# 32 inverse square roots per row half on GpSimd: one power instruction replaced by an integer seed, a cubic correction and a Newton step

## The reference, cut to what matters

```python
def l2norm(t):
    return t / jnp.maximum(jnp.linalg.norm(t, axis=-1, keepdims=True), 1e-12)
...
def attn_layer(x, Wqkv, qs, ksc, Wo):
    qkv = x @ Wqkv
    q, k, v = jnp.split(qkv, 3, -1)          # 16 heads of 64
    q = l2norm(q) * qs
    k = l2norm(k) * ksc
    q = q * cos * scale + rotate_half(q) * sin * scale
    k = k * cos * inv + rotate_half(k) * sin * inv
    out = local_attention(q, k, v)           # windows of 32, each sees itself and the one before
    return out @ Wo

def ffn_layer(x, g, bln, W1, b1, W2, b2):
    xn = (x - mu) / jnp.sqrt(var + 1e-05) * g + bln
    hg = xn @ W1 + b1
    a, gate = jnp.split(hg, 2, -1)
    return a * jax.nn.gelu(gate, approximate=False) @ W2 + b2
...
for i in range(DEPTH):                       # 6
    x = attn_layer(shift_tokens(x), ...) + x
    x = ffn_layer(shift_tokens(x), ...) + x
```

## Time and profile before

| what | value |
|---|---|
| time, median of 3 runs | 4746.68 us (4745.28 to 4752.33) |
| time of the profiled execution | 4743.42 us |
| its span, first to last instruction | 4741.6 us |
| mean granted TensorE clock | 0.957 |
| busy: PE, PEld, DVE, ACT, POOL | 87%, 59%, 62%, 55%, 70% |
| L908, the power: 192 instructions | 1044.0 us, 5438 ns each |

### The profile page before, as it was taken

One profiled execution on the slowest core, in us unless ns is written; L12 is line 12 of the kernel. 1 busy time (PEld: TensorE's weight loads), 2 busy tenths in 40 slices (PEclk: granted clock), 3 DMA queues, 4 the chain that ended last, 5 costly groups with the idle time before them and its releaser, 6 DMA issues. The chain is left out here.

```text
span 4741.6 us, 161504 instructions
## 1 busy us (share of the span) xinstructions
PE 4145.7 (87%) x67078; PEld 2784.5 (59%) x67078; DVE 2917.3 (62%) x4217; ACT 2627.4 (55%) x4417; POOL 3317.3 (70%) x1514
## 2 busy tenths in 40 slices
PE   5878788779999999999999999999999999999994
PEld 2434344356666666666666666666666666666663
DVE  5565656556666666666666666666666666666664
ACT  2535354446556556666556555656566555655562
POOL 0000000189889888988888889988898888888891
PEclk8989888899999999999999999999999999999997
DMA  0000000112222222222222222222222222222222
GB/s 27 2 15 2 15 16 2 41 45 56 65 70 74 54 69 65 71 56 65 65 69 63 56 65 73 75 51 69 65 72 57 62 65 69 63 56 65 69 73 71
DMA packets 284546, 258.84 MB, mean 55 GB/s; under 512 B 122871, under 2 KB 258508, under 8 KB 271148
## 3 DMA queue, kind: packets, MB, share of 16 engines
q1 hardware_dynamic: 283820, 248.14, 19.5%
HBM read 117.63 MB, written 29.77 MB: 31 GB/s over the span
## 5 line engine op out<-in xcount | busy, mean ns | idle before, releaser
L783 DVE TENSOR_TENSOR products<-bank_d,table 128x1024 f32<-128x1024 f32 x772 | 937.9, 1215 | 722.5 <-ACT sq L610 696.5
L908 POOL TENSOR_TENSOR rnorm<-clamped,minus_half 128x32 f32<-128x32 f32 x192 | 1044.0, 5438 | 16.0
L903 POOL TENSOR_TENSOR products<-products 128x2048 f32<-128x2048 f32 x192 | 870.7, 4535 | 152.0 <-DVE products L783 152.0
L409 PE MATMUL bank_d<-w_qkv,xT 128*128 128x512 f32 x1544 | 806.4, 625 | 19.6 <-DVE products L783 14.7
L610 ACT ACTIVATE sq<-bank_d 128x512 f32<-128x512 f32 x772 | 467.9, 606 | 478.7 <-PE bank_d L409 468.6
L926 POOL TENSOR_TENSOR qk_rot<-products,rnorm 128x2048 f32<-128x2048 f32 x192 | 695.5, 3622 | 14.9 <-POOL rnorm L908 14.5
L870 POOL MEMSET ident<- 128x128 f32 x1 | 0.2, 205 | 917.1 <-POOLq L1044 917.1
L781 DVE TENSOR_REDUCE ss<-sq 128x16 f32<-128x1024 f32 x386 | 468.6, 1214 | 232.5 <-ACT sq L610 232.5
L933 POOL TENSOR_TENSOR prob<-prob,inv_sum 128x1024 f32<-128x1024 f32 x192 | 365.1, 1901 | 187.5 <-DVE inv_sum L763 187.5
L1471 DVE TENSOR_REDUCE part_max<-s_max 128x1 f32<-128x512 f32 (+3 forms) x768 | 398.5, 554 | 151.2 <-PE s_max L1220 100.5
L455 PE MATMUL bank_a<-ident,qk_rot 128*128 128x128 f32 x3072 | 414.7, 291 | 76.8 <-issue 64.7
(11 more groups left out here) (158 smaller groups left out, 7216.9 us busy)
## 6 DMA issues: line engine op xcount, KB each, us to landing
v_back<-v SPq DMA_DIRECT2D x96, 768.0 KB, 5.4
w_qkv<-in_Wqkv_dram SPq DMA_DIRECT2D x25, 1024.0 KB, 5.1
v_back<-v SPq DMA_DIRECT2D x192, 128.0 KB, 5.4
w_qkv<-in_Wqkv_dram SPq DMA_DIRECT2D x25, 512.0 KB, 5.4
xs<-x_layers SPq DMA_DIRECT2D x194, 64.0 KB, 2.1
w_o<-in_Wo_dram SPq DMA_DIRECT2D x24, 512.0 KB, 5.5
xr<-x_layers SPq DMA_DIRECT2D x96, 128.0 KB, 2.2
x<-x SPq DMA_DIRECT2D x96, 128.0 KB, 1.8
```

The costliest lines, as they stand in the source:

```text
L409: nc.tensor.matmul(bank[:, :], xT[:, P * a:P * (a + 1)], w_qkv[:, col:col + 512], start=True, stop=True).then_inc(d_filled if i < 8 else a ...
L783: nc.vector.tensor_tensor(products[:, a, head:head + 8, :, :].rearrange("p h r (o d) -> p h r o d", o=2), bank[:, :].rearrange("p (h r d) ...
L903: link(nc.gpsimd.tensor_tensor(products[:, a, :, 0, :], products[:, a, :, 0, :], products[:, a, :, 1, :], ALU.add))
L908: link(nc.gpsimd.tensor_tensor(rnorm[:, a, :], clamped[:, a, :], minus_half[:, :], ALU.pow))
```

## The change

`inverse_norms` gets a new body. The clamp stays. The power over 32 values of each row (L908) is replaced by eleven instructions over the same 32 values: a seed from the bits of the float (tensor_scalar on int32 views), a cubic correction (six instructions) and one Newton step (four instructions). Seven of the eleven take two tensors (tensor_tensor), four take one (tensor_scalar); all are linked one behind the other. `minus_half` shrinks to the two columns that `normalise_x1` still uses; its power (L915) stays.

```diff
-        minus_half = sb("minus_half", [P, 2 * HEADS])
+        root_t = sb("root_t", [P, 2 * HEADS])
+        root_u = sb("root_u", [P, 2 * HEADS])
+        minus_half = sb("minus_half", [P, 2])
...
             def inverse_norms(a):
 
-                link(nc.gpsimd.tensor_scalar(clamped[:, a, :], ss[:, a, :], FLT_MAX, 1e-24, ALU.min, ALU.max))
-                link(nc.gpsimd.tensor_tensor(rnorm[:, a, :], clamped[:, a, :], minus_half[:, :], ALU.pow))
+                x, r, t, u = clamped[:, a, :], rnorm[:, a, :], root_t[:, :], root_u[:, :]
+                tt, ts = nc.gpsimd.tensor_tensor, nc.gpsimd.tensor_scalar
+                link(ts(x, ss[:, a, :], FLT_MAX, 1e-24, ALU.min, ALU.max))
+                link(ts(r.bitcast(i32), x.bitcast(i32), -0.5, float(RSQRT_MAGIC), ALU.mult, ALU.add))
+
+                link(tt(t, x, r, ALU.mult))
+                link(tt(t, t, r, ALU.mult))
+                link(ts(u, t, 0.375, -1.25, ALU.mult, ALU.add))
+                link(tt(u, u, t, ALU.mult))
+                link(ts(u, u, 1.0, 1.875, ALU.mult, ALU.add))
+                link(tt(r, r, u, ALU.mult))
+
+                link(tt(t, x, r, ALU.mult))
+                link(tt(t, t, r, ALU.mult))
+                link(ts(t, t, -0.5, 1.5, ALU.mult, ALU.add))
+                link(tt(r, r, t, ALU.mult))
```

More of the change, by code:

```diff
@@ L914, in normalise_x1 @@
                 nc.gpsimd.tensor_scalar(neg_mean[:, :], mean_var[:, :, 0], -1.0, 1.0, ALU.mult, ALU.mult)
-                link(nc.gpsimd.tensor_tensor(rstd[:, :], var_eps[:, :], minus_half[:, 0:2], ALU.pow))
+                link(nc.gpsimd.tensor_tensor(rstd[:, :], var_eps[:, :], minus_half[:, :], ALU.pow))
                 for a in range(2):
```

## The result

The changed kernel takes 4714.5 us, the median of 5 runs (4698.62 to 4720.53), against 4745.88 us (4742.41 to 4752.33, 5 runs) before. The ratio is 0.9929, 95% interval 0.9909 to 0.9948: faster by 0.7%. The forecast was 4723 and the range 4703 to 4742.

What follows compares the result with a forecast made beforehand. TensorE waits for `xn` behind GpSimd's power in three steps of four, with ScalarE's exponential chain close behind. Steady steps 15.5 plus ends 8.4 make 23.9 us: 4743.4 to 4719.5, plus 3.3 for the median, 4723; range 4703 to 4742.

Steps and rivals of the forecast that it cites:

- The cost of the eleven: GpSimd, per half: eleven linked instructions sum to 3.54 us against 5.52 for the power, saving 1.98 us.
- `xn` ended last: Steady steps: the chain over ScalarE's second exponential, without GpSimd, is only 0.38 us shorter than the one through `xn`.
- The gain of a steady step: Steady steps gain only ScalarE's idle time before `yT`: 16.5 us over 92 steps, taken as 15.5.
- Half 1 gains nothing in the steps: Steady steps: half 1 ends 1.98 us earlier but nobody waits for it there; gain 0.
- Filling and draining: TensorE's waits for `qk_rot` and `xn` at the beginning and end shrink by 3.9, 1.8, 0.8 and 1.9, together 8.4 us.
- A: Rival: TensorE's whole stop for `xn` is won, 111.4 us plus 8.4, giving 4627; chance 0.07.
- B: Rival: only the ends are won, 8.4 us, because the second chain grows some 0.2 us a step; 4738; chance 0.07.
- C: Rival: slower, the eleven outlast the power from 0.50 us mean distance; 4829, or about 4960 with a slow seed; chance 0.10.

Runs made afterwards that it cites:

- half 0 alone: Changed kernel, but half 1 keeps the power and only half 0 uses the seed and its corrections; 0.9938 of the kernel before.
- the root made 4.88 and 5.53 us long: Changed kernel plus four or six linked two-input scratch instructions per half; against the kernel before 0.9933 with four (4.88 us), 1.0008 with six (5.53 us).
- the seed alone: Changed kernel without the cubic correction and the Newton step, in both halves; 4697.6 us, 0.9902 of the kernel before.
- the moved table load: One-element exponential between squares of chunks 5 and 6 makes ScalarE load its table there; 0.9751 on the change, 0.9989 on the kernel before.
- half 1 alone: Changed kernel, but half 0 keeps the power and only half 1 uses the seed and its corrections; 0.9986 of the kernel before.

## Why the prediction was right, point by point

**The cost of the eleven.** Right to 0.01 us: 3.55 measured, 3.54 summed, with 0.335 for a two-input instruction and 0.30 for the others. The seed was the open price and costs nothing extra.

**`xn` ended last, by a few tenths of a us.** The prediction said 0.38 us for its step; start to start it is 4.03 - 3.54 = 0.49 there, and 0.34 to 0.43 in the medians. Shown from four sides: half 0 alone, the root made 4.88 and 5.53 us long, the seed alone, and the moved table load with and without the power.

**The gain of a steady step is the idle time before `yT`.** The mechanism was right and the size low, and this is the term to mend: 0.7 us a turn were summed, 22.8 us over 21 turns were measured, 1.09 a turn. The steps p = 1 and p = 2 gained 0.33 and 0.43 us, where the idle time before `yT` in such steps of the kernel before is 0.22 and 0.32 (medians; 0.38 in the step of the earlier trace rows). The missing 0.1 us a step is in how the idle time is counted. It runs from the recorded end of the second exponential, and a `yT` that has nothing to wait for starts 0.09 us before that end, 0.96 us after the exponential's start. The kernel before shows this in its steps p = 0 (median 0.96), and has 1.28, 1.37 and 1.29 us in p = 1, 2 and 3. Taken from the start of the exponential to chunk 9, the 92 steps of the loop stood 25.2 us above 3.53 us each before and stand 2.9 above it after: 22.3 us, against the 16.5 of idle time. What is left up to 1.09 x 23 = 25 us is smaller than the scatter of the starts of the turns.

**Half 1 gains nothing in the steps.** Shown by half 1 alone, with 37.15 us in p = 1 and 2.

**Filling and draining.** 6.5 us were summed for the fill. Up to the ninth add 6.55 were measured, and the agreement is partly luck: the last four of these steps are a turn of the loop, and at 1.09 us for it the fill itself is near 5.5. For the drain 1.9: TensorE's last wait for `qk_rot` fell from 2.76 us to 1.16, and from the start of the last table to this point it took 16.85 us and not 18.82. The row of the last three steps, +1.8 us, hides it in the table above; it holds a start of a turn, and the steps around such a start vary.

**The rivals.** A, the whole stop won, didn't come: 96.9 us of waits went, 67.2 came back in their place. B, only the ends, didn't either. C needed a mean distance of 0.50 us; it was 0.32.

**What is left of the difference.** The profiled pair differs by 26.6 us and the sum was 23.9. In the pair the front, which the change doesn't touch, was 3.2 us slower after; in the profiles of these kernels its first add starts between 935.92 and 946.62 us. So the terms that the change touches gave 29.8 and not 23.9: the steady steps some 9 us more over 23 turns, the fill 1 less, and the last three steps 1.8 us longer where they should have been 1 shorter. That the pair's 26.6 comes so near the sum is in part the slower front, and luck. The medians differ by 31.4 us with an interval of 25 to 43 and the sum lies 1 us below it. The forecast of 4723 is 8 us above the median, and the steady term is what it lacks.

## What to carry to other kernels

The length of a wait is not its worth. Before a wait is priced, follow the consumer's queue to the next place where it meets another engine, and look there for the idle time that this engine had to spare; that margin is the gain, here 0.4 of 1.65 us. Measure the margin from start to start: the idle time that is printed came out 0.1 us too small. And two chains that end 0.4 us apart have to be shortened together: the replaced power alone gave 0.7%, the moved table load alone 0.1%, the two together 2.5%.

## What the runs showed of the hardware

- A linked chain of small GpSimd instructions costs 0.30 us (one input) or 0.335 us (two inputs) from start to start at 128x32, and 0.08 to 0.09 us of it is the link. An int32 view costs the same, 217 against 216 ns. The power costs (5438 - 704) / 30 = 158 ns more for each further element of a row, while the eleven go from an estimated 3.1 us at 2 elements (0.28 each) to 3.55 at 32. With 0.79 us for the power at 2 elements (0.704 and the link), the eleven pay from an estimated 18 elements of a row on. The Trainium skill advises against elementwise work on GpSimd (GPSIMD Engine Reference, section 4.1); for these 32 elements no run moved the work to VectorE, and so it was not tried.
- Each start of a turn of the loop costs TensorE a stop of 2.5 to 3.3 us (22 starts). Before the change the profile names nothing that it waits for; after it, it puts 9 of the 22 stops down to `qk_rot`, but to that of half 1, while these transposes wait for half 0 only; in the one shown here it had ended 0.9 us before TensorE went on. The windows of the changed kernel just before and just after such a start, the column after the five engines being the granted clock, which is at its lower level of 1.2 GHz (0.50) once TensorE works again:

```profile
2306.50:2309.40 2.90, 0.00 (x0) 0.00 (x0) 2.48 (x3) 0.39 (x1) 2.06 (x2) 0.63 0.01 3
2309.50:2312.50 3.00, 3.00 (x15) 3.00 (x16) 0.75 (x5) 1.42 (x3) 3.00 (x1) 0.50 0.18 52
```

  The 16 transposes after it take 3.5 us in the median of the 22 turns and not 2.0. Together some 4.5 us a turn, and this stop is the longest single one in the loop. The steps p = 3 and p = 0 beside it take together between 77.3 and 82.2 us in this profile, more than the stop itself varies; what else varies there stays open. Over 22 turns the 79.64 to 80.52 us above make 19 us between profiles of like kernels, and the start of the first add, 935.92 to 946.62, another 11. That the 20 us between runs of one kernel come from these two was not shown, since each kernel has one profile.
